# A gated cross-attention block on one core: the rounding of the attention output goes from GpSimd to VectorE, the low parts of q and k from VectorE to GpSimd

## The reference, cut to what matters

```python
ln_out = _ln(hidden_states, ln_w, ln_b)
q  = _ln(_fp8_linear_pertensor(ln_out, wq,  ...), qln_w,  qln_b)    # 16 heads of 128
k  = _ln(_fp8_linear_pertensor(ln_out, wk,  ...), kln_w,  kln_b)    # 8 groups
qx = _ln(_fp8_linear_pertensor(ln_out, wqx, ...), qxln_w, qxln_b)
kx, vx = split(cond @ w_kv_x.T)
core = softmax(q  @ k.T  * scale) @ v
xout = softmax(qx @ kx.T * scale) @ vx
cat  = concatenate([core, xout])
catq = fp8_roundtrip(bfloat16(clip(cat / proj_smooth, -448, 448)))  # what magic and the add/subtract do
out  = catq @ wproj.T * (proj_in_scale * proj_w_scale)
```

## Time and profile before

| | us |
|---|---|
| median of three runs | 847.89 |
| the profiled execution, first to last instruction (its span) | 845.5 |
| PE busy | 767.8 |
| DVE busy | 624.1 |
| ACT busy | 475.0 |
| POOL busy | 458.4 |

### The profile page before, as it was taken

How to read it: one execution, slowest core, us unless ns; L and a number is a source line. 1 busy time by engine, 2 the same in 40 slices (tenths; PEclk the granted TensorE clock), 3 DMA queues, 4 the chain that set the end, 5 groups by cost and what they waited for, 6 DMA issues and landing times.

```text
span 845.5 us, 17655 instructions
## 1 busy us (share of the span) xinstructions
PE 767.8 (91%) x5307; PEld 635.1 (75%) x5307; DVE 624.1 (74%) x1330; ACT 475.0 (56%) x1266; POOL 458.4 (54%) x592
## 2 busy tenths in 40 slices
PE   3649999999997999999899999999997695999996
PEld 2547888888886888888778888878874563777775
DVE  7887887888884788888588887887877783444444
ACT  3647677777664567777466667776664241222221
POOL 3555666766663666667466666767665423322220
PEclk9769999999997899999999999999998896999999
DMA  6400010010010001000100010000000012666661
GB/s 201 143 25 7 20 51 1 26 52 1 26 28 27 1 27 41 11 2 26 53 1 26 3 50 2 26 1 1 2 2 0 1 64 75 182 199 190 182 197 59
DMA packets 44753, 42.97 MB, mean 51 GB/s; under 512 B 3973, under 2 KB 43642, under 8 KB 44666
## 3 DMA queue, kind: packets, MB, share of 16 engines
q1 hardware_dynamic: 43130, 36.62, 14.2%
q0 software_dynamic: 1536, 5.28, 2.3%
HBM read 39.52 MB, written 2.37 MB: 50 GB/s over the span
## 4 chain that ended last, share of the span: by engine, by line
PE 77%; DVE 9%; issue 5%; POOL 3%; ACT 3%; SPq 1%; DMA 1%; DVEq 0%; POOLq 0%; ACTq 0%
PE proj_ps L1372 13%; PE aux_ps L1427 11%; PE s_ps L1409 10%; PE out_ps L1633 8%; PE aux_ps L1442 8%; PE pT_ps L1418 6%; PE aux_ps L1391 5%; PE proj_ps L1379 5%; PE work_ps L1625 3%; PE work_ps L1647 2%; PE aux_ps L1337 2%; PE work_ps L1615 1%; DVE firsts L1241 1%; POOL rstd L517 1%; DVE rank L1243 1%
## 5 line engine op out<-in xcount | busy, mean ns | idle before, releaser
L745 ACT ACTIVATE p_sb<-s_ps,negmax 128x256 f32<-128x256 f32 x256 | 118.4, 472 | 62.8 <-DVE negmax L1035 61.9
L1372 PE MATMUL proj_ps<-wT,xq 128*128 128x128 f32 (+1 forms) x1024 | 140.0, 292 | 11.8 <-issue 11.7
L525 POOL TENSOR_SCALAR p_sb<-p_sb,rsum 128x256 f32<-128x256 f32 x256 | 120.6, 485 | 50.3 <-DVE rsum L1040 49.8
L1372 PEld LDWEIGHTS proj_ps<-wT,xq 128*128 128x128 f32 x1024 | 129.2, 200 | 15.2 <-issue 12.8
L1046 DVE COPY pT_sb<-pT_ps 128x512 f32<-128x512 f32 x128 | 87.7, 685 | 67.6 <-PE pT_ps L1418 67.6
L1409 PE MATMUL s_ps<-kT,qT 128*128 128x256 f32 x768 | 117.3, 296 | 11.7 <-DVE kT L1031 7.5
L1427 PE MATMUL aux_ps<-pT_sb,v_sb 128*128 128x512 f32 x256 | 122.5, 601 | 2.7 <-DVE pT_sb L1046 2.7
L532 POOL TENSOR_TENSOR y_bf<-y_bf,mg_bf 128x512 bf16<-128x512 bf16 x64 | 86.1, 1346 | 68.9 <-DVE mg_bf L1057 68.9
L1409 PEld LDWEIGHTS s_ps<-kT,qT 128*128 128x128 f32 x768 | 99.2, 193 | 18.0 <-DVE kT L1031 8.1
L702 ACT ACTIVATE sq<-proj_ps 128x768 f32<-128x768 f32 x64 | 51.9, 811 | 90.5 <-PE proj_ps L1379 90.5
L517 POOL TENSOR_TENSOR rstd<-var,minus_half 128x6 f32<-128x6 f32 x64 | 85.6, 1338 | 7.3 <-POOL var L513 3.9
(11 more groups left out here) (163 smaller groups left out, 1388.1 us busy)
## 6 DMA issues: line engine op xcount, KB each, us to landing
w_up<-in_L_ffn_gate_up_proj SPq DMA_DIRECT2D x32, 384.0 KB
w_down<-in_L_ffn_down_proj SPq DMA_DIRECT2D x32, 192.0 KB
wp_raw<-in_L_xattn_wproj SPq DMA_DIRECT2D x16, 256.0 KB, 2.8
w_raw<-in_L_xattn_wq SPq DMA_DIRECT2D x8, 256.0 KB, 2.6
w_raw<-in_L_xattn_wqx SPq DMA_DIRECT2D x8, 256.0 KB, 3.2
w_raw<-in_L_xattn_w_kv_x SPq DMA_DIRECT2D x16, 128.0 KB, 3.2
rows_dram<-xs SPq DMA_DIRECT2D x1, 1288.0 KB
x_sb<-in_x SPq DMA_DIRECT2D x4, 256.0 KB, 3.4
```

What stands on the lines that cost most here:

```text
L525: ins = nc.gpsimd.tensor_scalar(p_sb[:, r, st, :], p_sb[:, r, st, :], rsum[:, r, st:st + 1], 1.0, ALU.mult, ALU.mult)
L745: ins = nc.scalar.activation(p_sb[:, r, st, :], s_ps[:, r % 2, st, :], ACT.Exp, bias=negmax[:, r, st:st + 1], accum_out=psum_row[:, r, st: ...
L1372: nc.tensor.matmul(dst, xq[:, s.b, ty, c, tt * P:(tt + 1) * P], wT[:, s.gpar, part, c, bank * 512 + at:bank * 512 + at + width], start=(c ...
```

## The change: what it does

The add and the subtract that round `cat` go from POOL's `round_cat` to the end of DVE's `magic`. The three subtractions that make low parts go from DVE to POOL: TX stands behind `rstd_of(0)` and ahead of `p_norm(0)`, TQ and TK stand at the end of a step, behind `p_norm(3)`. The semaphore `magic_ready` goes; ACT, DVE and PE wait for `catq_ready`, now counted once per rounding. Sizes, types and the values computed stay.

```diff
@@ POOL @@
-            def round_cat(s, ty):
-
-                pool.wait_ge(magic_ready, s.n * 2 + (ty + 1))
-                nc.gpsimd.tensor_tensor(yc_bf[:, ty, :], yc_bf[:, ty, :], mg_bf[:, ty, :], ALU.add
-                                        ).then_inc(catq_ready, 1)
-                pool.wait_ge(catq_ready, s.n * 4 + (2 * ty + 1))
-                nc.gpsimd.tensor_tensor(catq[:, s.par, ty * HPG:(ty + 1) * HPG, :].rearrange("p a b -> p (a b)"),
-                                        yc_bf[:, ty, :], mg_bf[:, ty, :], ALU.subtract).then_inc(catq_ready, 1)
+            def qk_lo(s, x):
+
+                pool.wait_ge(qk_hi_ready[x], s.n + 1)
+                full, (hi, lo) = qk_parts(x)
+                nc.gpsimd.tensor_tensor(lo, full, hi.bitcast(F32), ALU.subtract).then_inc(qk_lo_ready[x], 1)
...
-                    if s := at(2):
-                        round_cat(s, 0)
                     if s := at(0):
                         rstd_of(s, 0)
                         if s.first:
                             quant_sub(1)
                     if s := at(1):
+                        qk_lo(s, "TX")
+                    if s := at(1):
                         p_norm(s, 0)
                         p_norm(s, 1)
-                    if s := at(2):
-                        round_cat(s, 1)
...
                         p_norm(s, 2)
                         p_norm(s, 3)
+                    if s := at(0):
+                        qk_lo(s, "TQ")
+                        qk_lo(s, "TK")
@@ ACT @@
-                wait(act, magic_ready, s.n * 2 + (ty - 1))
+                wait(act, catq_ready, s.n * 2 + (ty - 1))
@@ DVE @@
...
             def magic(s, ty, f):
                 dve.wait_ge(aux_free[f.bank], f.drained)
-                wait(dve, catq_ready, s.n * 4 + 2 * (ty - 1))
+                at = s.n * 8 + 4 * ty
+                wait(dve, catq_ready, s.n * 2 + (ty - 1))
...
                 nc.vector.tensor_scalar(mg_bf[:, ty, :], mg_bf[:, ty, :], 2.0 ** -6, 24.0, ALU.max, ALU.mult
-                                        ).then_inc(magic_ready, 1)
+                                        ).then_inc(round_chain, 1)
+                dve.wait_ge(round_chain, at + 3)
+                nc.vector.tensor_tensor(yc_bf[:, ty, :], yc_bf[:, ty, :], mg_bf[:, ty, :], ALU.add
+                                        ).then_inc(round_chain, 1)
+                dve.wait_ge(round_chain, at + 4)
+                nc.vector.tensor_tensor(catq[:, s.par, ty * HPG:(ty + 1) * HPG, :].rearrange("p a b -> p (a b)"),
+                                        yc_bf[:, ty, :], mg_bf[:, ty, :], ALU.subtract).then_inc(catq_ready, 1)
...
                         maxes(s, 1)
-                        qk_lo(s, "TX")
                         recip(s, 0)
...
                         magic(s, 0, s.fill("Vs"))
-                    if s := at(0):
-                        qk_lo(s, "TQ")
-                        qk_lo(s, "TK")
                     if s := at(1):
                         evac_pT(s, 3)
@@ PE @@
-                pe.wait_ge(catq_ready, s.n * 4 + 4)
+                pe.wait_ge(catq_ready, s.n * 2 + 2)
```

More of the change, by code:

```diff
@@ L223, in flamingo_kernel @@
         round_chain = sem("round_chain")
-        magic_ready = sem("magic_ready")
         catq_ready = sem("catq_ready")
@@ L1025, in scaled @@
                     ALU.mult).then_inc(qk_normed, 1)
[L1027 to L1031, removed]
             def maxes(s, r):
@@ L1049, in magic @@
                 dve.wait_ge(aux_free[f.bank], f.drained)
-                wait(dve, catq_ready, s.n * 4 + 2 * (ty - 1))
+                at = s.n * 8 + 4 * ty
+                wait(dve, catq_ready, s.n * 2 + (ty - 1))
                 nc.vector.tensor_scalar(yc_bf[:, ty, :], y_bf[:, ty, :], FP8_MAX, -FP8_MAX, ALU.min, ALU.max
                                         ).then_inc(round_chain, 1)
-                dve.wait_ge(round_chain, s.n * 4 + (2 * ty + 1))
+                dve.wait_ge(round_chain, at + 1)
                 nc.vector.tensor_scalar(mg_bf[:, ty, :].bitcast(U16), yc_bf[:, ty, :].bitcast(U16), 0x7F80, None,
                                         ALU.bitwise_and).then_inc(round_chain, 1)
-                dve.wait_ge(round_chain, s.n * 4 + (2 * ty + 2))
+                dve.wait_ge(round_chain, at + 2)
                 nc.vector.tensor_scalar(mg_bf[:, ty, :], mg_bf[:, ty, :], 2.0 ** -6, 24.0, ALU.max, ALU.mult
-                                        ).then_inc(magic_ready, 1)
+                                        ).then_inc(round_chain, 1)
[5 more added lines that the diff above has]
+                                        yc_bf[:, ty, :], mg_bf[:, ty, :], ALU.subtract).then_inc(catq_ready, 1)
             def add_acc(s, f):
```

## The result

The changed kernel took 898.62 us, the median of four runs (894.87 to 899.23), where the kernel before took 848.59 (four runs, 847.05 to 850.7). The ratio is 1.0579, with a 95% interval from 1.0545 to 1.0613: slower by 5.8%. The profiled execution has a span of 893.0 us, against 845.5.

A forecast was written before the change was run, and what follows sets the result against it. PE was taken to bound the kernel, through late arrivals. A walk of one step gave 1.35 us of stall; steps 31.0 + 9.0 + 2.0, start +1.5, end -3.0 made +40.5 on 845.5: span 886.0, median 888.4 us, range 865 to 912.

The forecast's parts named there:

- The two places of a step: PE stalls 1.35 us at `scores` 2: 0.6 from TX behind the power, 0.75 from DVE's late start on the squares.
- TX behind the power: POOL's TX subtraction, 1.16 us, starts after the power for rstd and makes `scores` 2 0.6 us late.
- DVE late on the squares: POOL's TQ and TK subtractions hold up DVE's `magic(0)` and rounding, so `sums(0)` starts 0.75 us later.
- TK and `scores` 0: At the first scores of a step, TK's low part ends 0.15 us later on POOL; not counted in the sum.
- The steps: Attention steps: 23 x 1.35 = 31.0 us, 5 with a group's first block 9.0, 2 between loop turns 2.0.
- Start: First step: TQ and TK stand behind POOL's last `quant_sub`, so PE's first scores come later, +1.5 us.
- End of the attention: PE's two waits for `catq` shrink as DVE does the last roundings in place of POOL, -3.0 us.
- The second half of a step: `magic(1)` has 1.1 us more on DVE beside POOL's `p_norm` 0 and 1, but margin takes it; counted as nothing.
- only the place behind the power counts: Rival, chance 0.16: `sums(0)` starts as before, so ordinary steps cost only 0.6 us; time 867.5 us.
- TX would be hidden on POOL: Rival, chance 0.05: TX is hidden behind PE's own work, leaving only the end's gain of -3.0; 844.9 us.
- POOL's subtraction takes 1.54: Part of a rival, chance 0.13: with DVE another 0.5 late for `scaled(1)`, 28 steps cost 0.88 more; 913 us.
- The clock: Other part of the 0.13 rival: PE's granted clock falls after stalls; stalls of 1.35 us judged shorter than earlier idle stretches.

The follow-up runs named there:

- e2: The changed kernel, but after the first block POOL subtracts TQ and TK over 8 of 512 columns, TX in full; 866.79 us.
- e1: The changed kernel, but after the first block POOL subtracts TX over only 8 of 512 columns; 878.68 us.
- e3: The changed kernel with all three POOL subtractions over 8 of 512 columns after the first block; 843.63 us.
- f2: Against the kernel before, only the rounding's add and subtract moved to DVE, all three low parts left on DVE; 855.38 us, ratio 1.0083.
- g1: The kernel before with only the last block's roundings moved from POOL to DVE; 847.32 us, ratio 0.9972.
- f1: The changed kernel with the TX subtraction back on DVE behind the row maxima; TQ and TK stay on POOL; 878.38 us.
- f3: Against the kernel before, only the three low parts moved to POOL, the rounding left on POOL; 906.8 us, ratio 1.0709.

## Why the prediction was right, and what was mis-sized

Forecast 888.4 us in a range of 865 to 912, measured 898.62. Direction and mechanism held; the sum was 7 us short (a span of 893.0 against 886.0). The other 3.2 are the median's distance from the profiled span: 2.4 before, 5.6 now, since the profiled execution was the fastest of the four. Term by term:

- **The two places of a step: right.** PE waits at `scores` 2 for POOL 27 times, 38.8 us in all, as said. e2 takes away one place and e1 the other, and e3 both; with both gone nothing is left.
- **TX behind the power: 0.6 forecast, 0.82 measured.** The subtraction takes 1.27 us, not 1.16, and `scores` 2 start 0.23 after its end, a hand-over for which the walk had nothing; its 0.05 between the power and TX was not there. What was mis-sized is the line drawn through rows of bf16 inputs: "so fp32 costs hardly more". The estimate worked out in the prediction from the figure in the Trainium skill, "GPSIMD Engine Reference", section "Performance versus the Vector engine", was 1.28, and the trace agrees with it.
- **DVE late on the squares: 0.75 forecast, 0.95 measured.** The walk was right place by place: POOL's TQ first, DVE's third instruction held, the add in the gap, TK held for a moment, the subtract held until 0.55 after TK's end (510.42 against 509.87). The 0.2 came at its start: TQ took 1.29, not 1.2, and DVE's add ended 2.79 after `project(0)`, where the walk had 2.6. From there to TK's end it was 1.13, with 1.1 in the walk. DVE's own two prices were right: 0.41 and 0.68 forecast, 0.43 and 0.69 where nothing held them (f2).
- **TK and `scores` 0: counted at nothing.** The walk let TK end 0.15 later; `scores` 0 start 3.98 after `project(0)`, where it was 3.57. In the change the larger stall behind it covers this; e1 shows it bare.
- **The steps: mis-sized, and most of the error.** From `project(1)` to `project(1)` the 30 steps grew from 557.65 to 605.30 us: 47.65, where 42 was forecast. The 23 came to 37.3 instead of 31.0; away from the loop turns the three kinds measured 1.31, 1.73 and 1.76 more, and I had put 1.35 for all, from one step's margin. The 5 with a group's first block came to 9.0 as forecast (18.72 to 20.56 in one). The two at a loop turn came to 0.2 and 1.1, 1.0 each forecast.
- **Start: 1.5 forecast, 1.53 measured,** by the second step's `project(1)`. PE's first wait for scores grew from 5.13 to 6.69.
- **End of the attention: -3.0 forecast, -1.68 measured** for all behind that stretch. The waits for `catq` gave back 4.0, more than forecast. But the rounding on DVE now stands ahead of the last copies of the probabilities, and PE's waits for those grew from 2.7 to 5.4; g1, which has this edit alone, shows the same 2.8. I had not walked the last step.
- **The second half of a step, counted at nothing: right for this kernel,** since the 1.78 lost at `scores` 2 is the step's 1.75. It was right only because PE's stall is the larger; e1 shows 0.2 a step as soon as TX's stall goes, and f2 some 0.37 a step with no other edit.
- **The rivals.** That only the place behind the power counts (867.5) is excluded by f1, which has nothing behind the power and is still 3.6% over before. That TX would be hidden on POOL is excluded by the difference of f1 and the change. That POOL's subtraction takes 1.54 is not borne out: TX took 1.27.
- **The clock, in part.** In the ordinary steps it stayed at 1.00, as in the window above. Behind the second loop turn it fell, where the earlier trace rows have 1.00 before the change. PE waited 3.34 us for TX at `scores` 2 there, far more than the 1.35 that the prediction set against both idle stretches:

```profile
452.00:456.00 4.00, 0.75 (x6) 0.76 (x7) 2.85 (x7) 3.41 (x13) 3.67 (x5) 1.00 0.00 0
456.00:460.00 4.00, 4.00 (x23) 4.00 (x23) 3.45 (x8) 0.14 (x1) 1.05 (x3) 0.58 0.00 0
```

  The 0.58 is a mean of the two levels, 1.2 and 2.4 GHz. That step took 20.93 us instead of 17.72. The 3.2 more are 1.5 over what its neighbours lose; I put this to the clock, and no run took it away. It is one of the 23 steps. The step behind the first turn took 20.30 instead of 20.82, with the clock down in both kernels.

## What to carry to other kernels

A step may look nearly neutral in the busy times of two engines and still cost 1.7 us, because what counts is where the moved instruction lands in its new engine's order: find the chain that PE waits for last (here squares, variance, power, scaling), and keep everything else off the engine that carries it. An instruction that stands where its engine waits anyway, like TX on DVE, costs nothing there, and moving it away gives nothing. And before work is put on GpSimd, look at what VectorE does beside it with operands in SBUF alone: here the two took turns, at 1.94 us a step.

## What the runs showed of the hardware

- **Which VectorE instructions POOL holds up.** Beside a two-operand POOL instruction, DVE's bf16 scaling with one input and an immediate (128x512) took 1.27 us instead of 0.29, and the subtract of two SBUF operands 1.65 instead of 0.69. The prediction read the turns as holding "when both read two operands from SBUF"; its walk let the one-input instruction wait all the same, without a row for it. The runs show that the rule is wider than I wrote it. DVE instructions with an operand in PSUM, and the sum of squares, were not held. In f3, beside POOL's TQ, TK, add, `catq` and TX instructions (493.57 to 494.86, 495.14 to 496.42, 496.37 to 497.53, 497.61 to 498.77, 500.52 to 501.78), DVE has:

```profile
493.74 1.28 DVE L1062 TENSOR_SCALAR mg_bf<-mg_bf 128x512 bf16<-128x512 bf16 x1
495.98 0.69 DVE L1051 COPY pT_sb<-pT_ps 128x512 f32<-128x512 f32 x1 [0.96 <-PE pT_ps L1419]
496.58 0.94 DVE L1023 TENSOR_REDUCE ss<-sq 128x6 f32<-128x768 f32 x1
...
498.17 0.68 DVE L1015 TENSOR_TENSOR wpT<-aux_ps,wpT 128x512 fp32r<-128x512 f32 x1
...
500.67 0.96 DVE L1032 TENSOR_TENSOR qk_tok<-proj_ps,rstd 128x768 f32<-128x768 f32 x1 [1.09 <-POOL rstd L517]
```

  Only the first, which ran beside TQ, is longer than elsewhere; the sum of squares and the three that have an operand in PSUM are not. The Trainium skill, "SBUF — State Buffer", section "Who interferes with whom", has the same division: VectorE contends with GpSimd in its two-port modes, which its `tensor_scalar` can enter, or with two inputs in SBUF, and not with one SBUF input outside those modes. The trace agrees, with 1.27 against 0.29 and 0.68 against 0.68.
- **The time of one POOL instruction with two operands.** 128x512 took 1.27 us with fp32 inputs (TX) and 1.16 with bf16 inputs (the add in f3), both beside nothing that held them; 8 columns of fp32 took 0.20 (e2).
- **The hand-over to PE went by the place and not by the engine.** POOL's TK ended at 509.87 and `scores` 0 began 0.06 later; behind DVE's TK it had been 0.05. POOL's TX ended at 515.02 and `scores` 2 began 0.23 later; before the change, where PE waited for DVE's TX, it was 0.24, from 425.89 to 426.13:

```profile
425.21 0.68 DVE L1031 TENSOR_TENSOR qT<-qk_f,qT 128x512 fp32r<-128x512 f32 x1
```

  Why `scores` 2 takes longer to begin than `scores` 0 was not tried.
